# A buffer for each of the first twelve pages, and the last product of a use behind the next one's first

## The reference

```python
q = _apply_rope((x @ wq).reshape(...), cos, sin)      # k likewise; v = x @ wv
scores = einsum('bqhd,bkhd->bhqk', q, k) / sqrt(32) + causal_mask
x = _layernorm(x + (softmax(scores) @ v) @ wo)
gate, up = x @ (gate_t * gate_s[:, None]).T, x @ (up_t * up_s[:, None]).T   # 3584 channels
x = _layernorm(x + (silu(gate) * up) @ (down_t * down_s[:, None]).T)
```

## Time and profile before

| | |
|---|---|
| median of three runs | 1923.5 us |
| the profiled execution | 1922.45 us |
| its span | 1920.7 us |
| mean granted clock of TensorE | 0.987 |
| PE, DVE, ACT, POOL busy | 95%, 60%, 40%, 26% |
| DMA, mean over the span | 110 GB/s |

### The profile page before, as it was taken

One profiled execution on the slowest core, in us unless ns is written; L12 is line 12 of the kernel. 1 busy time (PEld: TensorE's weight loads), 2 busy tenths in 40 slices (PEclk: granted clock), 3 DMA queues, 4 the chain that ended last, 5 costly groups with the idle time before them and its releaser, 6 DMA issues.

```text
span 1920.7 us, 27817 instructions
## 1 busy us (share of the span) xinstructions
PE 1831.2 (95%) x10592; PEld 892.0 (46%) x10592; DVE 1144.4 (60%) x2028; ACT 773.3 (40%) x1166; POOL 503.7 (26%) x999
## 2 busy tenths in 40 slices
PE   5989999999999987989999999999999999999997
PEld 2644655555555532434444444444444444444443
DVE  4877768677767763446444544756544544546645
ACT  3444434444434434445343344342453433334321
POOL 0354546456536555230000000212300000001204
PEclk8989999999999998999999999999999999999999
DMA  5644224433324297546132132349332312214201
GB/s 172 139 111 96 54 73 125 92 77 108 98 51 112 78 217 191 181 175 201 62 105 95 55 110 73 137 141 197 143 116 71 110 65 89 77 55 154 88 12 77
DMA packets 228021, 210.61 MB, mean 110 GB/s; under 512 B 183857, under 2 KB 184113, under 8 KB 227889
## 3 DMA queue, kind: packets, MB, share of 16 engines
q1 hardware_dynamic: 227024, 208.45, 38.1%
q10 hardware_dynamic: 864, 0.39, 0.1%
HBM read 133.03 MB, written 39.85 MB: 90 GB/s over the span
## 4 chain that ended last, share of the span: by engine, by line
PE 85%; DVE 6%; issue 2%; DMA 2%; SPq 2%; POOL 2%; ACT 2%; DVEq 0%; POOLq 0%; ACTq 0%
PE bank L856 34%; PE bank L871 20%; PE bank L762 18%; PE bank L810 4%; PE bank L774 3%; PE bank L798 3%; PE bank L821 2%; SPq L1339 1%; PE bank L777 1%; DVE row_max L1040 1%; DMA p_tiles<-xT 1%; DVE xT_parts L1004 1%; DVE stack_rows L1034 0%; DMA x_forms_spill<-x_parts 0%; DVE up_blocks L1140 0%
## 5 line engine op out<-in xcount | busy, mean ns | idle before, releaser
L856 PE MATMUL bank<-x_forms,weight_forms 128*128 128x512 f16 x3136 | 711.0, 380 | 24.3 <-DVE up_blocks L1140 9.6
L856 PEld LDWEIGHTS bank<-x_forms,weight_forms 128*128 128x128 f16 x3136 | 305.3, 98 | 402.9 <-issue 19.3
L871 PE MATMUL bank<-w_down,hid 128*128 128x512 f16 x1792 | 413.2, 379 | 3.1 <-DVE hid L1157 3.1
L922 ACT ACTIVATE p_tiles<-bank 128x512 f32<-128x512 f32 (+1 forms) x352 | 192.6, 556 | 285.6 <-PE bank L798 283.4
L871 PEld LDWEIGHTS bank<-w_down,hid 128*128 128x128 f16 x1792 | 175.0, 98 | 215.1 <-DVE hid L1157 4.0
L1040 DVE TENSOR_REDUCE row_max<-bank 128x1 f32<-128x384 f32 (+3 forms) x352 | 219.3, 635 | 85.6 <-PE bank L777 84.7
L1245 POOL TENSOR_TENSOR acc<-acc,down_scale 128x1024 f32<-128x1024 f32 x16 | 38.6, 2410 | 769.2 <-DVE acc L1178 769.2
L762 PE MATMUL bank<-wq_parts,xT_parts 128*128 128x256 f16 x1536 | 216.4, 275 | 3.4 <-DVE wq_parts L1004 3.3
L762 PE MATMUL bank<-wo_parts,att_parts 128*128 128x512 f16 x768 | 191.5, 382 | 2.0 <-DVE row L1089 1.4
L1211 POOL TENSOR_SCALAR_AFFINE_SELECT p_tiles<-p_tiles 128x128 f32<-128x128 f32 (+2 forms) x352 | 139.2, 404 | 206.6 <-ACT p_tiles L922 204.9
L762 PEld LDWEIGHTS bank<-wq_parts,xT_parts 128*128 128x128 f16 x1536 | 144.7, 98 | 47.7 <-issue 9.0
(11 more groups left out here) (99 smaller groups left out, 1767.2 us busy)
## 6 DMA issues: line engine op xcount, KB each, us to landing
w_page<-gateT SPq DMA_DIRECT2D x56, 512.0 KB, 4.5
w_page<-upT SPq DMA_DIRECT2D x56, 512.0 KB, 4.4
w_page<-downT SPq DMA_DIRECT2D x56, 512.0 KB, 4.5
x_forms_spill<-x_parts SPq DMA_DIRECT2D x56, 256.0 KB, 2.5
att_spill<-att_made SPq DMA_DIRECT2D x64, 128.0 KB, 2.2
att_parts<-att_spill SPq DMA_DIRECT2D x16, 512.0 KB, 3.4
x_row<-x_spill SPq DMA_DIRECT2D x16, 512.0 KB, 3.3
out<-acc SPq DMA_DIRECT2D x16, 512.0 KB, 2.7
```

Source lines behind the costliest of these rows:

```text
L856: t = nc.tensor.matmul(strassen[bank_set(use)][to][:, :], w_form[:, use % 4, A_FORMS[a_form], k * P:(k + 1) * P], xF[:, :, B_FORMS[b_form] ...
L871: t = nc.tensor.matmul(to[:, :], hid[g % 2][:, c, a, i % 2, i // 2 * P:(i // 2 + 1) * P], w_down[:, g % 2 * GC + c, cols], start=g == grou ...
L922: nc.scalar.activation(p32[j][:, h0:h0 + heads, :], bank[5 + m % 2][:, 0:heads * n].rearrange("p (h c) -> p h c", c=n), ACT.Exp, scale=SCO ...
```

## The change

It has two parts.

**Pages.** `FIRST` has a new order: x first, then two wq pages, then four of wkv, then the rest as before. In a batch's first unit the q group now stands ahead of the kv group. Each of the twelve pages has its own buffer and its own semaphore: five in `p_tiles`, seven in the space of `wo_parts`, whose own pages must now wait until all twelve are split. SP waits for nothing before the first fourteen pages. The first two loads of x rows for the residual (L1319), which stood right behind the first page, now come after the last split of wo. The source of wkv is laid out so that a page is one block.

**Products.** `PRODUCT_ORDER` lists all products; for uses 4 to 54 except 27 the last product of a use changes places with the first product of the next. `PRODUCT_N` gives the number of each product in that order, and every wait on the count of products uses it.

```diff
-FIRST = (("wkv", 0, 0), ("x", 0, 0), ("wkv", 0, 1), ("wkv", 0, 2), ("wkv", 0, 3), ("wq", 0, 0), ("wq", 0, 1),
-         ("x", 0, 1), ("x", 0, 2), ("x", 0, 3), ("wq", 1, 0), ("wq", 1, 1))
+FIRST = (("x", 0, 0), ("wq", 0, 0), ("wq", 0, 1), ("wkv", 0, 0), ("wkv", 0, 1), ("wkv", 0, 2), ("wkv", 0, 3), ("x", 0, 1), ("x", 0, 2), ("x", 0, 3), ("wq", 1, 0), ("wq", 1, 1))
...
+PRODUCT_ORDER = [(use, i) for use in range(USES) for i in range(NPR)]
+for use in range(4, USES - 1):
+    if use != 2 * NF - 1:
+        at = PRODUCT_ORDER.index((use, NPR - 1))
+        PRODUCT_ORDER[at:at + 2] = reversed(PRODUCT_ORDER[at:at + 2])
+PRODUCT_N = {which: n + 1 for n, which in enumerate(PRODUCT_ORDER)}
...
-        before = n - 4 if n < NFIRST else n - 2 if n >= NFIRST + 2 else -1
+        before = n - 2 if n >= NFIRST + 2 else NFIRST - 1 if what == "wo" else -1
...
-            items = [i for t in range(NT) for i in (("kv", u // UNITS, t), ("q", u, t))]
+            items = [i for t in range(NT) for i in (("q", u, t), ("kv", u // UNITS, t))]
...
-    row = [("x1_store", tile - 2)] if 1 < tile < TILES - 2 else []
+    row = [("x1_store", tile - 2)] if 1 < tile < TILES - 2 else [("split_lo", "wo", 0, KD - 1)] if tile < 2 else []
...
-            after += [ended(use, i - 1) if i else ended(use - 1, NPR - 1)] if use or i else attention
+            n_back = PRODUCT_N[use, i] - 2
+            after += [ended(*PRODUCT_ORDER[n_back])] if n_back >= 0 else attention
...
-        first_page = [p_all[:, i * D:(i + 1) * D] for i in range(4)]
+        first_page = [p_all[:, i * D:(i + 1) * D] for i in range(5)] + [
+            wo_p[:, :, :, :].rearrange("p a k c -> p (a k c)").bitcast(F32)[:, i * D:(i + 1) * D] for i in range(NFIRST - 5)]
...
-            if what == "wkv":
-                return wkv[:, 2 * j:2 * j + 2, :]
+                return wkv[j]
...
-                    on.wait_ge(s_prod, NPR * use + (1, 5, 6)[k])
+                    on.wait_ge(s_prod, PRODUCT_N[use, (0, 4, 5)[k]])
...
-                    on.wait_ge(s_hi, before + 1)
-                    on.wait_ge(s_lo, before + 1)
+                    if n >= NFIRST + 2:
+                        on.wait_ge(s_hi, n - 1)
+                        on.wait_ge(s_lo, n - 1)
```

More of the change, by code:

```diff
@@ L97, with bank_set @@
 NPR = len(PRODUCTS)
+def bank_set(use):
+    return use % 2 if use > 3 else 0
+PRODUCT_ORDER = [(use, i) for use in range(USES) for i in range(NPR)]
[4 more added lines that the diff above has]
+PRODUCT_N = {which: n + 1 for n, which in enumerate(PRODUCT_ORDER)}
 BLOCKS = [(0, 0), (0, 1), (1, 1), (1, 0)]
@@ L208, in attention_plan @@
         at = ranks[what, b, j]
-        before = n - 4 if n < NFIRST else n - 2 if n >= NFIRST + 2 else -1
+        before = n - 2 if n >= NFIRST + 2 else NFIRST - 1 if what == "wo" else -1
         last = [loads[n - 1]] if n else []
         put(SY, at, .4, "page_load", what, b, j, moves=PAGE_MOVES,
-            after=[("page_load", *w) for w in last] + ([("split_lo", *loads[before])] if before >= 0 else []))
+            after=[("split_lo", *loads[before])] if before >= 0 else [])
         put(SC, at, 1.04, "split_hi", what, b, j, after=[("page_load", what, b, j)] + [("split_hi", *w) for w in last] + (
@@ L567, in block_kernel @@
         s_const, s_scale, s_set = sem("const_dma"), sem("scale_dma"), sem("const_set")
-        s_first = [sem(f"first_page_dma{i}") for i in range(4)]
+        s_first = [sem(f"first_page_dma{i}") for i in range(NFIRST)]
         s_page = [sem(f"page_dma{i}") for i in range(2)]
@@ L889, in scalar_program @@
                     on.wait_ge(arrived, 16 * times)
+                    if which[0] == "wo":
+                        on.wait_ge(s_lo, NFIRST)
                     if which[0] == "x" and which[1]:
@@ L1407 @@
         "wq": heads_split(g["attn_wq"], NH).reshape(2, KD // 2, P, UNITS, UH * HD).transpose(3, 0, 2, 1, 4),
-        "wkv": chunked(np.concatenate([heads_split(g["attn_wk"], NKV), g["attn_wv"]], 1)),
+        "wkv": np.concatenate([heads_split(g["attn_wk"], NKV), g["attn_wv"]], 1).reshape(KD // 2, 2, P, -1).transpose(0, 2, 1, 3),
         "wo": chunked(g["attn_wo"]),
```

16 lines of the change are left out of this document (7 added, 9 removed).

## The result

| | before | after |
|---|---|---|
| runs | 6 | 6 |
| median | 1922.62 us | 1899.8 us |
| lowest to highest | 1918.05 to 1925.29 | 1896.21 to 1902.77 |
| the profiled execution | 1922.45 us | 1897.28 us |
| its span, PE busy, PE idle | 1920.7, 1831.2, 89.5 | 1895.5, 1823.7, 71.8 |

What follows compares the result with a forecast made beforehand. PE, busy 1831.2 of 1920.7 us, was taken as the bound. From 1922.45 us, 12.3 for attention (13.8 less 3 for DVE, plus 1.5 for POOL) and 5.4 for feed-forward gave 1904.8, said as 1905; range 1897 to 1915.

Steps and rivals of the forecast that it cites:

- Start, 13.8 us: Program start: pages issued without waits let PE finish six projection groups at 36.2 us instead of 50.0, 13.8 us earlier.
- The clock, in the range at 2.9 us: Start: PE, beginning in pieces with pauses, may be at its lower clock at 20 us, costing up to 2.9 us.
- Rival 4: Start: SP held up, pages landing in another order or behind the first transpose; lead 8 us, time 1911; chance 0.10.
- Given back by DVE, 3 us: Up to the first k scores: DVE, nearly full, can't follow PE's whole lead; 3 us off leaves 10.8.
- wrong if the lead at the first k scores is above 13: First k scores, expected at 72 to 73 us: a lead below 8 or above 13 us would show the forecast wrong.
- POOL's stop, 1.5 us of gain: After the scales' all-reduce: PE's 6.03 us wait behind POOL's 7.54 us stop shrinks to 4 to 5; gain 1.5 us.
- Feed-forward, 5.4 us net: Product swap: ten waits totalling 8.0 us and one of 0.17 go; waits of 1.85 and 0.95 come; net 5.4 us.
- Rival 2: Feed-forward: the swap wins nothing, forms and casts ahead of sums being late in sparse stretches; time 1910; chance 0.08.
- Rival 3: Dense feed-forward: paired down products delay sums at odd uses; slower, 1926 us or more; chance 0.04.
- the band of 1900 to 1908.5: Whole kernel: the forecast's own narrower band of times around 1905 us; chance 0.50.
- rival 5: Attention: POOL's stop is hidden wholly and DVE keeps up; time 1897 us; chance 0.11.

Runs made afterwards that it cites:

- experiment 5: The changed kernel with its twelve buffers, but the old order of pages and of q and kv groups: 1896.25 us, ratio 0.985.
- experiment 6: The changed kernel with its new page order, but four buffers used in turn as before: 1917.84 us, ratio 0.9968.
- experiment 10: The changed kernel with the scales' all-reduce moved to where POOL waits anyway (near 242 us), a small addition right behind it: 1887.27 us, ratio 0.9825.
- the control: The changed kernel run again, unchanged, beside the later runs: 1898.15 us, ratio 0.9875.
- experiment 8: The changed kernel with all-reduce at program start, small all-reduce before and addition behind it, and later weight casts and forms of uses 29 and 33: 1893.37 us.
- experiment 11: The changed kernel with the all-reduce where POOL waits anyway, plus later weight casts and forms of uses 29 and 33: 1885.54 us, ratio 0.9806.
- experiment 1: The changed kernel without the loop that swaps products, so the page part alone: 1905.2 us, ratio 0.9918.

## Why the prediction was right, and where its terms were off

- **Start, 13.8 us: right, 13.3.** PE began at 8.74 (said 8.65), the last kv quarter at 19.59 (said 18.0), six groups ended at 36.49 (said 36.2). The mechanism is the buffers, not the order (experiments 5 and 6); how much of it needs the row loads out of the way too is open. The clock, in the range at 2.9 us, did not fall: after 16 us every group runs at the upper level. Rival 4 did not come: SP was never held up.
- **Given back by DVE, 3 us: the step that failed; nothing was given back.** The lead grew from 13.3 to 14.3 at the first k scores. From the end of six groups to the first k scores, before and after, in the order of columns of the earlier trace rows:

```profile
49.81:83.22 33.41, 31.04 (x250) 22.07 (x248) 29.28 (x62) 10.71 (x14) 5.51 (x6) 1.00 0.64 136
```
```profile
36.49:68.95 32.46, 30.96 (x250) 22.29 (x249) 28.98 (x60) 10.74 (x15) 4.36 (x6) 1.00 0.62 141
```

  It is nearly the same work for both engines (on DVE three splits of wo stand where three of wq did), and DVE is as full as before (29.28 of 33.41 us, then 28.98 of 32.46). I took that fullness as a limit on the lead. But the lead was won ahead of this stretch, where DVE had room: up to its start DVE was busy 20.23 of 49.81 us before and 24.12 of 36.49 after, with eleven and with fifteen splits done. So DVE came to the stretch as early as PE did, and PE waits for it there for 0.24 us at most. The window from 50 to 100 us, which I had read before, can't show this: DVE is busy only 40.45 us in it now (before 45.06), but mainly because POOL's stops hold the whole core up; in experiment 10, without them, it is 44.42. The mark "wrong if the lead at the first k scores is above 13" was met, on the good side.
- **POOL's stop, 1.5 us of gain: 1.1 by the lead, but not as I told it.** I saw one stop of 7.54 us. There are two around the all-reduce. Before, the first fell into a time in which POOL had to wait for DVE anyway (until 114.93 of 115.72 us). Now both do harm: PE stands 7.54 us for masks, not 4 to 5 (before 6.03, for an exponential of ACT). So the sign of the term is right by luck. Other waits in the same stretch shrank. What neither kernel's waits show is the clock behind them; taking both stops out of the way was worth 10.9 us (experiment 10), of which 6.7 in the control's trace and 7.5 in the changed kernel's are waits.
- **Feed-forward, 5.4 us net: the places all right, the price of a wait too low.** Ten waits went, 1.80 (said 1.85) and 0.88 (said 0.95) came, none arose in the dense stretches; idle time fell by 5.65. But a wait costs 0.16 to 0.20 us more than its idle time, and the stretch won 7.66. Experiments 8 and 11 show the two new waits to be the casts and forms, as worked out: moving these took 2.7 and 2.6 us off. Rivals 2 and 3 are out.
- **What is left of the 25.2 us:** 0.7 us before the feed-forward, with a transfer of maxima waited for 1.87 instead of 4.66 us, and 1.4 in its first uses at a higher clock (0.88 from 848 to 860 us, against 0.75 at the same work before). No part of the change is meant to touch either, and experiment 1, with the same attention, had the wait at 5.53. The sum of medians, 16.4 and 7.0, is a fairer size of the two parts.

Between the profiled executions the forecast was 7.5 us short (17.7 against 25.2): 4.0 for DVE, 2.3 for the feed-forward, 2.1 of the last point, less 0.5 for the start and 0.4 for the stop. Against the median it was 5.2 us short, just under the band of 1900 to 1908.5 and nearer to rival 5 (1897). Half of rival 5 is what came: DVE kept up, but POOL's stops were not hidden. The mechanism of the start and of the swap was right; that the total lies in the range is owed to a range wide enough for one false term of 3 us.

## What to carry to other kernels

A neighbour that is 90% busy in a stretch does not eat a lead that was won ahead of it, if the neighbour comes to the stretch as early as PE does: ask that first, and compare stretches by the work in them, not by fixed times. Price each short wait of PE at its idle time plus what the restart costs, which shows only as a longer busy row. And look at a rare instruction on GpSimd for its two stops; put it where that engine waits anyway, which here won half as much again as the feed-forward part of the change.
